# PixArt block with mixture of experts: weighing the context rows by three fp32r products instead of one f32 product

## What is computed

```python
q = (xq @ wq).reshape(b, sq, H, DH).transpose(0, 2, 1, 3)
k = (ctx @ wk).reshape(b, sk, H, DH).transpose(0, 2, 1, 3)
v = (ctx @ wv).reshape(b, sk, H, DH).transpose(0, 2, 1, 3)
scores = jnp.einsum("bhqd,bhkd->bhqk", q, k) / math.sqrt(DH)
attn = jax.nn.softmax(scores, axis=-1)
out = jnp.einsum("bhqk,bhkd->bhqd", attn, v)
return out.transpose(0, 2, 1, 3).reshape(b, sq, INNER) @ wo + bo
```

## Time and profile before

| | us |
|---|---|
| median of 3 runs | 2151.15 (2149.22 to 2152.4) |
| the profiled execution, its own time | 2138.83 |
| its span, first to last instruction | 2137.1 |
| its mean granted TensorE clock | 0.987 of 2.4 GHz |

### The profile page before, as it was taken

The page is one execution under the profiler, slowest core; times in us unless marked ns, Lnnn a source line. Parts: engine busy times, 40 slices in busy tenths (PEclk is TensorE's granted clock), DMA queues, the critical chain, the costliest instruction groups (busy, mean ns, idle before and its releaser), DMA issues. The chain is left out here.

```text
span 2137.1 us, 38900 instructions
## 1 busy us (share of the span) xinstructions
PE 2049.8 (96%) x11132; PEld 1347.9 (63%) x11132; DVE 1334.3 (62%) x3405; ACT 1392.3 (65%) x2665; POOL 1067.5 (50%) x1198
## 2 busy tenths in 40 slices
PE   6899999999999999999999999999999888899996
PEld 5455565655556555555555555656565548799996
DVE  4564657676767676767676766666656645466565
ACT  4566666666666666667676767676766656666663
POOL 1443444546464636363636373737372535465654
PEclk9999999999999999999999999999999999999998
DMA  4101111111111111112111111111112312122257
GB/s 133 45 29 41 50 35 50 46 50 45 49 44 49 44 49 44 49 44 54 44 49 44 49 44 49 44 49 44 52 47 69 98 44 59 40 67 66 73 180 217
DMA packets 136322, 127.36 MB, mean 60 GB/s; under 512 B 14665, under 2 KB 110569, under 8 KB 136234
## 3 DMA queue, kind: packets, MB, share of 16 engines
q1 hardware_dynamic: 127466, 109.11, 18.3%
q0 software_dynamic: 8768, 17.20, 2.4%
HBM read 86.63 MB, written 40.67 MB: 60 GB/s over the span
## 5 line engine op out<-in xcount | busy, mean ns | idle before, releaser
L1866 POOL TENSOR_TENSOR pr<-pr,sm 128x512 f32<-128x512 f32 x256 | 277.5, 1097 | 492.4 <-DVE sm L1419 492.4
L1095 ACT ACTIVATE kp<-ps 128x512 f32<-128x512 f32 x512 | 298.3, 600 | 182.1 <-PE ps L281 180.3
L816 PE MATMUL ps<-tt,V 128*128 128x512 f32 x768 | 381.8, 595 | 3.5 <-ACT tt L1095 3.5
L1409 DVE TENSOR_REDUCE mx<-ps 128x8 f32<-128x512 f32 x256 | 176.7, 690 | 313.3 <-PE ps L765 313.3
L1095 ACT ACTIVATE tt<-ps 128x512 f32<-128x512 f32 x512 | 274.9, 590 | 40.3 <-PE ps L795 40.3
L765 PE MATMUL ps<-kp,hf 128*64 128x256 f32 x2048 | 277.8, 393 | 7.2 <-DVE pr L1412 3.8
L281 PE MATMUL ps<-cT,M 128*128 128x512 f32 x768 | 261.8, 464 | 0.0
L765 PEld LDWEIGHTS ps<-kp,hf 128*64 128x64 f32 x2048 | 124.7, 136 | 197.3 <-DVE pr L1412 135.4
L1095 ACT ACTIVATE pt<-ps 128x512 f32<-128x512 f32 x256 | 153.5, 600 | 142.7 <-PE ps L777 142.7
L281 PE MATMUL ps<-hk,M 128*128 128x512 f32 x768 | 243.7, 440 | 1.9 <-DVE hk L1473 1.9
L922 PE MATMUL ps<-xT,wt 128*128 128x128 f32 (+1 forms) x1728 | 222.7, 279 | 5.7 <-ACT sl L1268 2.9
(11 more groups left out here) (228 smaller groups left out, 3498.1 us busy)
## 6 DMA issues: line engine op xcount, KB each, us to landing
mod<-emb_s SPq DMA_DIRECT2D x96, 256.0 KB, 4.3
xr<-rows_s SPq DMA_DIRECT2D x144, 66.0 KB, 1.9
cb<-y_s SPq DMA_DIRECT2D x32, 256.0 KB, 5.2
x_in<-in_x_dram SPq DMA_DIRECT2D x16, 256.0 KB, 4.4
xn_s<-x_in SPq DMA_DIRECT2D x16, 256.0 KB, 2.0
res<-xn_s SPq DMA_DIRECT2D x16, 256.0 KB, 2.8
c_in<-in_ctx_dram SPq DMA_DIRECT2D x16, 256.0 KB, 4.8
y_s<-res SPq DMA_DIRECT2D x16, 256.0 KB, 2.1
```

The lines of the kernel that those rows point to most:

```text
L816: mm = nc.tensor.matmul(psO[:], Vw[a][:, g * HG + head_at(h), :], tt[:, h, :], start=(g == 0 and h == 0), stop=ends)
L1095: return nc.scalar.activation(o, i, ACT.Copy)
L1409: nc.vector.tensor_reduce(mx[:, p % 2, :], heads(psS[p % 2][:]), AX_X, ALU.max).then_inc(max_done, 1)
L1866: tensor(v, v, sm[:, p, :].unsqueeze(2).broadcast_to([P, HG, 64]), ALU.mult).then_inc(prob_done, 1)
```

## The change

The weighing of the context rows (units 2 and 3, for chunks 0 to 13) becomes three fp32r products: rows low times probabilities high, rows high times probabilities high, rows high times probabilities low.

- ACT's copy of the turned tile goes to `pt_hi` (fp32r). DVE gets a new operation, `turn_rest`: it subtracts `pt_hi` from psT into `pt_lo`. It stands ahead of `peak(p)` in the turn phases of slots 3 and 0.
- `turn(p)` for p over 0, and each other user of psT after tile 3, now waits for DVE's `pt_rest` instead of ACT's `pt_done`. The third product waits for `pt_rest` too.
- In those two slots one `total` stands in the turn phase instead of two: `total(0)` after peak 3, and `total(1)`, `(2)`, `(3)` at h = 0, 1, 2.
- POOL splits `c_tm` once a round (`split_context`, two operations over 128x512) in slot 2 at h = 4, after `router_out`. SP loads `c_tm` earlier, behind the load of x in slot 1.
- The new buffers share their place in SBUF with the experts' raw weights; the semaphore `identity` is merged into `made`.

```diff
+        def in_halves(i, u):
+            return u >= 2 and not (isinstance(i, int) and i >= NC - 1)
+        def halves_count(i, u, p):
+            return 4 * (2 * (i - 1) + u - 2) + p + 1
+        def turned(i, u, p):
+            return (pt_rest, halves_count(i, u, p)) if in_halves(i, u) else (pt_done, 4 * seq(i, u) + p + 1)
...
 # SP, round_
+                if ok(i - 1):
+                    if not first(i - 1):
+                        sp.wait_ge(t_done, 8 * (seq(i - 1, 3) + 1))
+                    sp.dma_start(c_tm[:], ctx_v[i - 1]).then_inc(ld_cm, 16)
                 if ok(i - 2):
                     load_ahead(i, 1, 7)
...
 # PE, turn
-                if not (isinstance(n, int) and n < 1):
+                if p:
+                    wait(turned(i, u, p - 1))
+                elif not (isinstance(n, int) and n < 1):
                     pe.wait_ge(pt_done, n)
...
 # PE, weigh
+                if in_halves(i, u):
+                    if p == 0 and u == 2:
+                        pe.wait_ge(c_split, 2 * i)
+                    for k, of in enumerate((1, 0)):
+                        for s in range(2):
+                            rows = slice(64 * s, 64 * s + 64)
+                            nc.tensor.matmul(pst[s][:], c_hl[rows, of, p, :], pt_hi[rows, p % 2, :], start=k == 0, stop=False)
+                    pe.wait_ge(pt_rest, halves_count(i, u, p))
+                    for s in range(2):
+                        rows = slice(64 * s, 64 * s + 64)
+                        nc.tensor.matmul(pst[s][:], c_hl[rows, 0, p, :], pt_lo[rows, p % 2, :], start=False, stop=True).then_inc(t_done, 1)
+                    return
...
 # ACT, turn_hi
-                copy(pt[:, p % 2, :], psT[:]).then_inc(pt_done, 1)
+                copy((pt_hi if in_halves(i, u) else pt)[:, p % 2, :], psT[:]).then_inc(pt_done, 1)
...
 # DVE
+            def turn_rest(i, u, p):
+                dve.wait_ge(pt_done, 4 * seq(i, u) + p + 1)
+                tensor(pt_lo[:, p % 2, :], psT[:], f32(pt_hi[:, p % 2, :]), ALU.subtract).then_inc(pt_rest, 1)
...
 # DVE, slot
+                early = 1 if last and in_halves(li, lu) else EARLY
                 for p in range(NT):
+                    if last and in_halves(li, lu):
+                        turn_rest(li, lu, p)
                     if here:
                         peak(i, u, p)
-                    if p >= 4 - EARLY and here:
-                        total(i, u, p + EARLY - 4)
+                    if p >= 4 - early and here:
+                        total(i, u, p + early - 4)
...
-                    if h < NT - EARLY and here:
-                        total(i, u, h + EARLY)
+                    if h < NT - early and here:
+                        total(i, u, h + early)
...
 # POOL
+            def split_context(c):
+                pool.wait_ge(ld_cm, 16 * (c + 1))
+                if not first(c):
+                    pool.wait_ge(t_done, 8 * (seq(c, 3) + 1))
+                tensor(c_hl[:, 0], c_tm[:], allone[:].unsqueeze(1).broadcast_to([P, NT, P]), ALU.mult).then_inc(c_split, 1)
+                pool.wait_ge(c_split, 2 * c + 1)
+                tensor(c_hl[:, 1], c_tm[:], f32(c_hl[:, 0]), ALU.subtract).then_inc(c_split, 1)
...
-                         2: ((2, 3, router_mul), (4, 3, router_out)),
+                         2: ((2, 3, router_mul), (4, 3, router_out), (4, 1, split_context)),
```

More of the change, by code:

```diff
@@ L119, in pixart_block_moe @@
         RAWS = 4
+        with ExitStack() as halves:
+            c_hl = sb("c_hl", [P, 2, NT, D], F32R, halves)
+            pt_hi, pt_lo = (sb(f"pt_{k}", [P, 2, CT], F32R, halves) for k in ("hi", "lo"))
         raw_1 = sb("raw_1", [P, RAWS, 6, P])
@@ L589, in round_ @@
                     load_mod(i, 1)
[L590 to L593, removed]
                 if ok(i):
@@ L695, in _ @@
             pe.wait_ge(consts, 3)
-            pe.wait_ge(identity, 2)
+            pe.wait_ge(made, 2)
             def setup(lo, hi):
@@ L989, in next_key @@
                         if last:
-                            for w in [(pt_done, 4 * seq(li, lu) + 4)] if bank is psT else [] if bank in psS else t_free(li, lu, 3 if bank is psH else 2):
+                            for w in [turned(li, lu, 3)] if bank is psT else [] if bank in psS else t_free(li, lu, 3 if bank is psH else 2):
                                 wait(w)
@@ L1024, in slot @@
                     if last:
-                        pe.wait_ge(pt_done, 4 * seq(li, lu) + 4)
+                        wait(turned(li, lu, 3))
                     turn4(psT, back1, lambda k: oT[:, k * P:(k + 1) * P])
@@ L1821, in _ @@
         def _(pool):
-            nc.gpsimd.memset(ident[:], 0.0).then_inc(identity, 1)
-            pool.wait_ge(identity, 1)
+            nc.gpsimd.memset(ident[:], 0.0).then_inc(made, 1)
+            pool.wait_ge(made, 1)
             nc.gpsimd.affine_select(out=ident[:], in_=ident[:], compare_op=ALU.not_equal, fill=1.0, base=0,
-                                    pattern=[[-1, P]], channel_multiplier=1).then_inc(identity, 1)
+                                    pattern=[[-1, P]], channel_multiplier=1).then_inc(made, 1)
             nc.gpsimd.memset(allone[:], 1.0).then_inc(made, 1)
@@ L1848, in number @@
                 pool.wait_ge(made, made_n[0])
-            made_n = [7]
+            made_n = [9]
             number(jj[:], [[1, 128]], 0, 0)
@@ L2013, in slot @@
                     for at, lag, stage in hooks:
-                        if at == h and ok(i - lag):
+                        if at == h and ok(i - lag) and (stage is not split_context or in_halves(i, 2)):
                             stage(i - lag)
```

6 lines of the change are left out of this document (3 added, 3 removed).

## The result

The changed kernel takes 2175.03 us (median of 4, 2173.44 to 2177.33) where the kernel before takes 2150.68 (2149.22 to 2152.40) in the same rounds of measuring: a ratio of 1.0114, 95% interval 1.0096 to 1.0131, so 24 us slower. The forecast was 2171.0, its range 2154 to 2186, with 0.82 on slower. One thing is needed to read all that follows: the kernel before takes about 2138.5 us in some measurements (on two chips) and 2151 to 2157 in others (on two further chips, and once on a chip that is not on record), so each kernel is compared only with the kernel before measured beside it.

The account below looks back on a forecast made before the run. The PE was taken to bound the rounds (busy 105.11 of 105.20 us). Slot 3 +1.53, slot 0 -0.03, slot 2 +0.1 made +1.6 a round for 12 rounds, plus 0.5 for round 2: +19.7, 2171 us, range 2154 to 2186.

Parts of the forecast that it names:

- The weighing, 0.90, and 17.9 us less work: Weighing pair on PE: 0.90 us instead of 1.06, saving 0.16 on each of 112 weighings, 17.9 us less PE work.
- The rival with unoverlapped halves: Weighings on PE: fp32r halves don't overlap, a weighing takes 1.6 us, some +70 us, 2221; chance 0.05.
- that with shown loads: Weighings on PE: weight loads show in every pass, a weighing takes 1.20 us, +33 us, 2184; chance 0.06.
- Turn 1, +0.61: Slot 3: turn 1 waits for DVE's subtraction of tile 0, a stall of 0.61 us that nothing hides.
- Turn 3, +0.85: Slot 3: ACT's chain bounds the stretch to the copy of tile 2, so turn 3 starts 0.85 us later.
- The GLU product, +1.53: Slot 3, second GLU product: 0.69 us from later scores of tile 3 plus 0.84 for one more total, +1.53.
- Slot 2, +0.1: Slot 2: GpSimd's split delays DVE's layer norm; PE may lose 0 to 0.65 us, taken as 0.1 a round.
- Slot 1, 0: Slot 1 of a round: no term in the forecast's sum, so no change.
- Round 1, 0: First round: no table load, 0.64 us saved against a stall of about 0.6, so 0.
- The signs named beforehand: Profile after: turn 1 waits some 0.6 us, turn 3 0.5 to 0.6, GLU product about 1.0; round about 106.8; PE busy some -18.
- only the wait on psT costs: Rival: DVE's tail in slot 3 shrinks elsewhere, leaving +0.5 us for 13 rounds, 2158; chance 0.13.
- That the waits are hidden: Rival: the saving stands and the waits are hidden, -17.9 us, 2133; chance 0.14.

Follow-up runs that it names:

- the kernel with the split alone: Kernel before with only GpSimd's split of the context rows and the moved load added; f32 weighings, no subtraction, totals as before: 2137.88 us beside 2138.42.
- the kernel with the totals put back: Changed kernel with the totals in the order of the kernel before, all else as changed: 2148.72 us beside 2138.42 for the kernel before.
- the waits alone: Changed kernel with one f32 product a sequence again; DVE's subtraction, its waits, late totals and GpSimd's split stay: 2164.51 us beside 2138.42 for the kernel before.
- the version with tile 0 of unit 3: Version with tiles 1 and 3 in halves and total 3 behind `glu_mul`, plus tile 0 of unit 3 in halves: 2139.65 us beside 2156.14 (kernel before).

## Why the prediction was right

- **The weighing, 0.90, and 17.9 us less work.** 0.89 to 0.90 in the steady rounds of nearly every trace. Alone it gave -17.2, but only 14.9 of that in the rounds, since one of the eight weighings is lost before the GLU product; that the whole came so near to 17.9 is in part luck. So the working's first step, that in the rounds every us that the PE saves is a us of the kernel, failed at that one place. The halves overlap in fp32r as in f32. The Trainium skill's rule (TensorE: Matmul & The Clock Gate, Part 3) that a load overlaps a running product only in another row group would, taken by itself and by the prediction's estimate, have made 1.20 of it; the measurement decides against it here. The rival with unoverlapped halves and that with shown loads are both out.
- **Turn 1, +0.61.** +0.67. The 0.06 is the PE's own start, 0.06 after DVE's end, and DVE's start, 0.10 after ACT's.
- **Turn 3, +0.85, bound by ACT.** +0.91, the same 0.06 carried along. First keys +0.53: +0.57.
- **The GLU product, +1.53.** +1.60. Of it 0.84 is the moved total (taken back: 0.79 and 0.85 gained) and the rest the late scores. That was the largest term, at a place where the PE waited already. What I had not seen is how long it waited: 0.64 us.
- **Slot 0, -0.03:** +0.03. **Slot 2, +0.1:** 0.00 to 0.02 in the loop. The delay that was feared did come, 1.8 us of the 2.6 that two operations could make, and fell just inside the 1.95 that were free; that it cost nothing was close.
- **Slot 1, 0:** wrong, +0.4 in the first profile and 0.5 in the two others. Without it a round is longer by 1.65, forecast 1.6; with it by 2.06 to 2.17.
- **Round 1, 0:** +0.5: 0.8 in slot 2 from the split beside the layer norm, which the working had only for the loop (the kernel with the split alone shows it), and -0.1 and -0.2 in the two turn phases behind it, where the stall of tile 0 and the saved weighings nearly cancel, as forecast. **Round 2, +0.5:** +0.4.
- **The signs named beforehand.** Turn 1 waits 0.61, turn 3 0.49, the GLU product 1.12, near what was named. The round is 107.26, not 106.8, and the PE's busy time fell by 12 us, not 18.

So in slots 3 and 0, on which the forecast rests, each term came within 0.1 us of what was measured. By the rounds the change costs 24.7 us: 4.1 of slot 1 (ten rounds at 0.41), 0.5 of round 1, 0.4 of round 2, and 19.7 for all else in rounds 3 to 14, where 19.2 was forecast. The whole came 4 us over the forecast because slot 1, which the working had set to nothing, is not nothing. The rival *only the wait on psT costs* is what the kernel with the totals put back shows: +10.3 where that rival said +7, so its price was near, and it is wrong because DVE's tail didn't shrink (in the changed kernel 8.37 us from the start of peak 3 to that of `glu_mul` where it was 7.50, which is the moved total's 0.84 and a little). That the waits are hidden is out by the waits alone, +26.

## What to carry to other kernels

A product made cheaper by splitting an operand pays only if the engine that makes the second part is out of the loop around the bank: here DVE's 0.69 us stood between a copy and the next turn, and where other work already filled that gap (before turn 2, and behind tile 3) it cost nothing. Split the tiles with slack and leave the others: here half of the tiles gave 0.7 us a round where all of them without any wait gave 1.1. Before adding work to a helper engine, look for the place where the bound engine starts right behind it: one total moved past that place was worth 0.8 us a round in the changed kernel, as much as the new wait. And when a helper's work costs nothing, look how much of the slack it used: here 1.8 of 1.95 us.

## What the runs showed of the hardware beyond that

- fp32r products on 64-row halves run beside each other: four of them take 0.57 us from start to start, the two that follow 0.32 to 0.33, against 1.06 for the f32 pair and 0.23 for one fp32r product of full height.
- A busy share of 99.9% (105.11 of 105.20) held 0.64 us a round in which PE stood. Start-to-start times against the same group elsewhere (0.46) show it, and so does the idle time of the weight loads (0.92 there, 0.24 once the wait is gone); the idle time of the products themselves doesn't.
- Two programs with identical instructions in a stretch differed by 0.4 to 0.5 us in when ACT's copy started behind PE's transposes. The changed kernel has it in nearly every round of the hardware loop in three profiles; the kernel with the same waits and f32 products never (that one was measured where the kernel before takes 2138 us). GpSimd issues four scatters ahead of that turn, the last of them 0.6 us before it in the changed kernel, 0.95 in the version with tile 0 of unit 3 (a delay of 0.15), 1.5 in the kernel before (none but in one round). But the waits alone have it at 0.6 without a delay, and round 15, written out, at 0.6 in the changed kernel without one. The cause stays open.
